# Attention scores: products over 96 stacked rows of the whole array in place of 64-row tiles

## What is computed

```python
x = x + tanh(g_xattn[0]) * L0_xattn(layernorm(x), ctx, mask, ...)
x = x + tanh(g_ffn[0])   * L0_ffn(layernorm(x), ...)     # mixture of 8 experts, top 2, and a shared one
x = x + tanh(g_xattn[1]) * L1_xattn(layernorm(x), ctx, ...)
x = x + tanh(g_ffn[1])   * L1_ffn(layernorm(x), ...)     # ternary weights

# in either attention, 16 heads of 16 numbers
Q = q @ Wq + bq;  K = ctx @ Wk + bk;  V = ctx @ Wv + bv
attn = softmax(Q K^T / 4 + mask);  out = (attn V) @ Wo + bo
```

## Time and profile before

| | |
|---|---|
| median of 3 runs | 1268.31 us (1262.6 to 1273.34) |
| the profiled execution's span | 1276.2 us |
| TensorE busy | 1203.0 us, 94% |
| VectorE busy | 998.5 us, 78% |
| ScalarE busy | 786.4 us, 62% |
| GpSimd busy | 673.1 us, 53% |
| share of the chain that ended last | PE 73%, DVE 10%, issue 7%, ACT 5%, POOL 4% |
| score matmuls (L832) in the two lines that the page has of q_hi's | 512 of them, mean 366 ns |

### The profile page before, as it was taken

The page is one execution under the profiler, slowest core; times in us unless marked ns, Lnnn a source line. Parts: engine busy times, 40 slices in busy tenths (PEclk is TensorE's granted clock), DMA queues, the critical chain, the costliest instruction groups (busy, mean ns, idle before and its releaser), DMA issues.

```text
span 1276.2 us, 27021 instructions
## 1 busy us (share of the span) xinstructions
PE 1203.0 (94%) x9168; PEld 1111.4 (87%) x9169; DVE 998.5 (78%) x2077; ACT 786.4 (62%) x1521; POOL 673.1 (53%) x772
## 2 busy tenths in 40 slices
PE   7999999989888999999799999999999999899998
PEld 6888888879878999999788888888899998788887
DVE  6888888866797676666668888887887788878887
ACT  4777677658554555555557767776444445677874
POOL 5333333333104555553777777730465466778885
PEclk8999999979899999999869999999999999999999
DMA  3221112023201333333533333302100000000000
GB/s 104 62 61 53 51 51 51 19 66 108 75 1 38 114 107 103 108 104 97 123 65 64 60 63 60 60 23 84 38 2 0 0 0 1 2 25 25 25 25 33
DMA packets 72319, 68.67 MB, mean 54 GB/s; under 512 B 26624, under 2 KB 64256, under 8 KB 72000
## 3 DMA queue, kind: packets, MB, share of 16 engines
q1 hardware_dynamic: 57936, 47.78, 12.5%
q0 software_dynamic: 12576, 18.62, 7.9%
q10 hardware_dynamic: 1744, 1.50, 0.4%
HBM read 44.00 MB, written 18.61 MB: 49 GB/s over the span
## 4 chain that ended last, share of the span: by engine, by line
PE 73%; DVE 10%; issue 7%; ACT 5%; POOL 4%; DMA 0%; ACTq 0%; DVEq 0%; POOLq 0%
PE PSUM L772 13%; PE PSUM L774 13%; PE PSUM L773 12%; PE PSUM L832 6%; PE PSUM L853 6%; PE PSUM L841 4%; PE PSUM L785 3%; PE PSUM L851 2%; PE PSUM L808 2%; PE PSUM L862 2%; POOL s_t_gh L2614 2%; PE PSUM L1914 1%; DVE s_a_q_lo L422 1%; ACT s_a_q_hi L677 1%; PE PSUM L2803 1%
## 5 line engine op out<-in xcount | busy, mean ns | idle before, releaser
L2164 POOL TENSOR_TENSOR s_f_h_lo<-s_f_h,s_f_h_hi 128x512 fp32r<-128x512 f32 x64 | 93.4, 1466 | 104.6 <-ACT s_f_h_hi L2108 104.0
L1337 POOL DMA_INDIRECT s_m_tile_x<-normed_x,s_tokens x78 | 95.7, 1227 | 77.0 <-DVE s_tokens L1628 55.5
L853 PEld LDWEIGHTS PSUM<-s_a_v_diagonal,s_a_prob_t 128*128 128x128 f32 x1024 | 128.4, 195 | 0.0
L853 PE MATMUL PSUM<-s_a_v_diagonal,s_a_prob_t 128*128 128x36 f32 x1024 | 127.4, 271 | 0.0
L1005 POOL DMA_INDIRECT s_x<-sorted_y,s_slots x60 | 95.1, 1586 | 50.2 <-DMA s_x<-sorted_y,s_slots 34.0
L454 DVE TENSOR_REDUCE s_a_row_max<-PSUM 128x8 f32<-128x640 f32 x128 | 104.4, 815 | 12.9 <-PE PSUM L832 10.3
L702 ACT ACTIVATE s_a_prob_t<-PSUM 128x640 f32<-128x640 f32 x128 | 89.4, 699 | 34.2 <-PE PSUM L841 33.4
L832 PE MATMUL PSUM<-s_a_kd,s_a_q_hi 64*128 64x320 f32 x512 | 92.8, 366 | 16.7 <-DVE s_a_q_lo L422 16.7
L461 DVE TENSOR_TENSOR s_a_less<-PSUM,s_a_row_max 128x640 f32<-128x640 f32 x128 | 105.0, 820 | 3.6 <-issue 0.2
L685 ACT ACTIVATE s_a_prob<-s_a_less 128x512 f32<-128x512 f32 x128 | 80.5, 629 | 41.8 <-DVE s_a_less L461 41.7
L2102 ACT ACTIVATE s_f_h<-PSUM,s_cols 128x512 f32<-128x512 f32 x64 | 44.0, 688 | 89.0 <-PE PSUM L774 88.3
(11 more groups left out here) (327 smaller groups left out, 4318.4 us busy)
## 6 DMA issues: line engine op xcount, KB each, us to landing
sorted_y<-s_m_tile_y SPq DMA_DIRECT2D x39, 256.0 KB, 2.1
s_a_kd<-s_a_k_parts SPq DMA_DIRECT2D x252, 20.0 KB
s_x<-x SPq DMA_DIRECT2D x16, 256.0 KB, 2.8
s_a_ctx<-ctx SPq DMA_DIRECT2D x32, 128.0 KB, 2.5
s_moe_raw<-moe_w SPq DMA_DIRECT2D x16, 256.0 KB, 3.4
normed_x<-s_m_xn SPq DMA_DIRECT2D x16, 256.0 KB, 3.2
y<-s_x SPq DMA_DIRECT2D x16, 256.0 KB, 2.1
s_late_raw<-moe_w SPq DMA_DIRECT2D x11, 256.0 KB, 2.8
```

Source lines behind the costliest of these rows:

```text
L853: last = pe.matmul(a.o_ps[:, 2 * c:2 * c + 2, :], a.prob_t[j % 2][:, c, :], v[:, j // BT, 0, 2 * c:2 * c + 2], start=False, stop=c == PC - ...
L1337: pool.indirect_dma_start(m.tile_x[n % 2][:, t, :], None, d["normed_x"], bass.IndirectOffsetOnAxis(ap=tokens[:, BT * n + t:BT * n + t + 1] ...
L2164: pool.tensor_tensor(f.h_lo[m % 4][:], f.h[m % 4][:], f.h_hi[m % 4][:].bitcast(F32), ALU.subtract).then_inc(f.h_split, 1)
```

## The change

1. **Layout.** `lay_out` permutes the columns of Wq and Wk (and their biases), so that four neighbouring partitions of a chunk hold the same row of its four head pairs.
2. **Stacks.** A new buffer `q_stack` has in 96 partitions three copies of a head pair's 32 rows: q_hi, q_lo, q_hi. `kd` has in the same 96 partitions k_hi, k_hi, k_lo, the two heads of a pair in columns of their own. The three products hi x hi, lo x hi and hi x lo are so one contraction over 96 rows. `q_stack` is filled by three DMAs of 256 KB a block from SyncE (`stack_queries`), two from q_hi and one from q_lo; `kd` by six DMAs of 40 KB instead of eight of 20 KB. q_hi and q_lo have one buffer each instead of two.
3. **Score.** Four matmuls a unit, each 96 rows, 128 queries, 160 columns (one head pair), in place of six. Only j = 0 waits for the stacks (one semaphore, nine DMAs).
4. **Keys two blocks ahead.** The keys are made two blocks ahead, the values still one ahead. The second block's keys are made in the opening. x is still loaded two blocks ahead.
5. **Order.** The bodies of all engines are reordered. TensorE's turn: tp(last,3), score 1, wv(last,2), transpose_x of the next, tp 0, score 2, wv(last,3), queries of the next, wv 0, score 3, tp 1, transpose_o of the last, a wait for the next block's q_lo, keys of the block after next, values of the next, tp 2, wv 1, score 0 of the next, and project of the last, which waits for both parts of the next block's value matrix and for the keys' parts. The `reach` of the loops on TensorE and ScalarE is 3, so two more blocks are unrolled.

The lines that carry it, left out: semaphore names, buffers' places in memory, the bodies of ScalarE and GpSimd.

```diff
+
+    row = np.arange(P) // 4
+    chunk_order = (2 * (np.arange(P) % 4) + row // HD) * HD + row % HD
+    by_pair = np.concatenate([m * P + chunk_order for m in range(KC)])
+    i = {**i, "L0_xattn_Wq": i["L0_xattn_Wq"][by_pair], "L0_xattn_Wk": i["L0_xattn_Wk"][by_pair],
+         "L1_xattn_Wq": i["L1_xattn_Wq"][:, by_pair], "L1_xattn_Wk": i["L1_xattn_Wk"][:, by_pair],
+         **{n: i[n][by_pair] for n in ("L0_xattn_bq", "L0_xattn_bk", "L1_xattn_bq", "L1_xattn_bk")}}
...
-                    self.kd = [sb(scope, n + f"kd{z}", [P, 2, KC, HPC // 2, CTXP], F32R) for z in two]
+                    self.kd = [sb(scope, n + f"kd{z}", [P, 2, HEAD_PAIRS, KC, CTXP], F32R) for z in two]
...
-        def spread_keys(engine, a, b, heads):
+        def spread_keys(engine, a, b, places):
             engine.wait_ge(a.k_split, b.count + 1)
-            for h in heads:
-                rows = slice(h * HD, (h + 1) * HD)
-                engine.dma_start(a.kd[b.z][rows, :, :, h % (HPC // 2), :].bitcast(F32),
-                                 a.k_parts[b.z][rows].bitcast(F32)).then_inc(a.kd_in[b.z], 16)
+            for h in places:
+                for copy, part in enumerate((0, 0, 1)):
+                    rows = slice(copy * PAIR_ROWS + h * HD, copy * PAIR_ROWS + (h + 1) * HD)
+                    engine.dma_start(a.kd[b.z][rows, h].bitcast(F32),
+                                     a.k_parts[b.z][h * P // 2:(h + 1) * P // 2, part].bitcast(F32)).then_inc(a.stacks_in[b.z], 16)
+
+        def stack_queries(engine, a, b):
+            stack = a.q_stack[b.z]
+            engine.wait_ge(a.q_round, b.count + 1)
+            for copy in (0, 2):
+                engine.dma_start(stack[copy * PAIR_ROWS:(copy + 1) * PAIR_ROWS].bitcast(F32), a.q_hi[:].bitcast(F32)).then_inc(a.stacks_in[b.z], 16)
+            engine.wait_ge(a.q_split, b.count + 1)
+            engine.dma_start(stack[PAIR_ROWS:2 * PAIR_ROWS].bitcast(F32), a.q_lo[:].bitcast(F32)).then_inc(a.stacks_in[b.z], 16)
...
                 late_rows = a.stage == 1 and not behind
-                if ahead and (a.stage or behind):
-                    ln_apply(b.next())
                 if a.stage and ahead == 0:
                     ffn_norm(0)
+                score_max(b, 1)
                 if behind:
                     normalise(b.last(), 2)
-                score_max(b, 1)
                 less_max(b, 1)
+                if ahead:
+                    x_residue(b.next())
                 if ahead > 1 and not late_rows:
                     ln_stats(b.next().next())
                 if a.stage and ahead == 1:
                     ffn_stats()
                 if a.stage and ahead == 0:
                     ffn_norm(1)
-                if ahead:
-                    keys(b.next())
-                if ahead:
-                    value_tails(b.next())
                 if behind:
                     normalise(b.last(), 3)
+                score_max(b, 2)
+                less_max(b, 2)
+                normalise(b, 0)
+                if ahead:
+                    q_residue(b.next())
                 if ahead > 1 and not late_rows:
                     ln_aggregate(b.next().next())
                 if a.stage and ahead == 1:
                     ffn_aggregate()
-                score_max(b, 2)
-                less_max(b, 2)
-                normalise(b, 0)
-                if ahead:
-                    x_residue(b.next())
+                score_max(b, 3)
                 if behind:
                     o_residue(b.last())
-                score_max(b, 3)
+                if ahead > 1:
+                    keys(b.next().next())
+                less_max(b, 3)
+                if ahead:
+                    value_tails(b.next())
+                if a.stage and ahead == 0:
+                    ffn_residue()
+                normalise(b, 1)
                 if late_rows:
                     ln_stats(second.next())
                     ln_aggregate(second.next())
                 if ahead:
-                    q_residue(b.next())
-                less_max(b, 3)
-                if a.stage and ahead == 0:
-                    ffn_residue()
-                if ahead:
                     score_max(b.next(), 0)
-                normalise(b, 1)
-                if ahead:
                     less_max(b.next(), 0)
                 if behind:
                     residual(b.last())
+                if ahead > 1:
+                    ln_apply(b.next().next())
...
                 if opens(a, b):
-                    act.wait_ge(first_steps, 2)
+                    act.wait_ge(a.first_k_ps, 1)
+                elif isinstance(b.n, int) and b.n == 0:
+                    act.wait_ge(a.v_ps, b.count + 1)
+                elif isinstance(b.n, int) and b.n == 1:
+                    act.wait_ge(a.first_k_ps, 2 + a.stage)
                 else:
-                    act.wait_ge(a.kv_ps, b.count + 1)
-                after(act, a.kd_in[b.z], 16 * HPC * (b.half + a.base // 2))
+                    act.wait_ge(a.v_ps, b.count)
+                after(act, a.stacks_in[b.z], 16 * STACK_DMAS * (b.half + a.base // 2))
                 for m in range(KC):
                     last = act.activation(a.k_parts[b.z][:, 0, m, :], k_bank(a, b)[:, m * CTXP:(m + 1) * CTXP], ACT.Identity,
                                           bias=cols[:, a.bk + m:a.bk + m + 1])
                 last.then_inc(a.k_round, 1)
 
...
             def q_rounded(b):
                 act.wait_ge(a.q_ps, b.count + 1)
+                if not (isinstance(b.n, int) and b.n == 0):
+                    stacked = b.last()
+                    act.wait_ge(a.stacks_in[stacked.z], 16 * STACK_DMAS * (stacked.half + a.base // 2 + 1))
                 for m in range(KC):
-                    last = act.activation(a.q_hi[b.z][:, m, :], q_bank(a, b)[:, m * SEQ:(m + 1) * SEQ], ACT.Identity,
+                    last = act.activation(a.q_hi[:, m, :], q_bank(a, b)[:, m * SEQ:(m + 1) * SEQ], ACT.Identity,
...
             def score(b, j):
                 u = UNITS * b.count + j
                 m, qt = j // BT, j % BT
-                pe.wait_ge(a.kd_in[b.z], 16 * HPC * (b.half + a.base // 2 + 1))
-                pe.wait_ge(a.q_split, b.count + 1)
+                if j == 0:
+                    pe.wait_ge(a.stacks_in[b.z], 16 * STACK_DMAS * (b.half + a.base // 2 + 1))
                 pe.wait_ge(a.masked, u + 1)
-                queries = (a.q_hi[b.z], a.q_lo[b.z], a.q_hi[b.z])
-                keys = (a.kd_hi[b.z], a.kd_hi[b.z], a.kd_lo[b.z])
-                for i in range(3):
-                    for c in range(2):
-                        rows = slice(c * P // 2, (c + 1) * P // 2)
-                        ps = a.scores[:, j % 2, c, 0:HPC // 2 * CTXP].rearrange("p (h n) -> p h n", n=CTXP)
-                        last = pe.matmul(ps, queries[i][rows, m, qt * P:(qt + 1) * P], keys[i][rows, m],
-                                         start=False, stop=i == 2, skip_group_check=True)
+                for p in range(HEAD_PAIRS):
+                    ps = a.scores[:, j % 2, p // 2, p % 2 * 2 * CTXP:(p % 2 + 1) * 2 * CTXP].rearrange("p (h n) -> p h n", n=CTXP)
+                    last = pe.matmul(ps, a.q_stack[b.z][0:STACK, p, m, qt * P:(qt + 1) * P], a.kd[b.z][0:STACK, :, p, m, :],
+                                     start=False, stop=True, skip_group_check=True)
                 last.then_inc(a.scores_ps, 1)
...
 
                 if ahead:
-                    pe.wait_ge(a.q_split, b.count + 3)
+                    pe.wait_ge(a.v_main, b.count + 3)
+                    pe.wait_ge(a.v_tail, b.count + 3)
+                    if ahead > 1:
+                        pe.wait_ge(a.k_split, b.count + 4)
                 else:
                     pe.wait_ge(a.y_done, b.count + 1)
...
                 if behind:
                     transpose_prob(b.last(), 3)
+                score(b, 1)
+                if behind:
                     weigh_values(b.last(), 2)
-                score(b, 1)
                 if ahead:
-                    keys_values(b.next())
-                if behind:
-                    weigh_values(b.last(), 3)
-                else:
+                    transpose_x(b.next())
+                if not behind:
                     pe.wait_ge(a.bias_step, 4 + 3 * a.stage)
                 transpose_prob(b, 0)
                 score(b, 2)
+                if behind:
+                    weigh_values(b.last(), 3)
                 if ahead:
-                    transpose_x(b.next())
+                    queries(b.next())
                 weigh_values(b, 0)
+                score(b, 3)
                 transpose_prob(b, 1)
-                score(b, 3)
                 if behind:
                     transpose_o(b.last(), 1)
                 if ahead:
-                    queries(b.next())
+                    pe.wait_ge(a.q_split, b.count + 2)
+                if ahead > 1:
+                    keys(b.next().next())
+                if ahead:
```

(7 more changed lines are left out.)

160 lines of the change are left out of this document (95 added, 65 removed).

## The result

The changed kernel takes 1420.81 us, the kernel before 1265.49 in the same runs (the 1268.31 above is the median of three of its four): a ratio of 1.1208 (95% interval 1.1162 to 1.1254). 1262 was forecast, with a range up to 1288.

A forecast was written before the change was run, and what follows sets the result against it. TensorE was taken to bound the turn, 15.08 us of work plus a 0.42 wait. Steady turns -12.7, last turns -2, openings +4.6 and clock +4 gave -6.1, so 1268.3 became 1262 us, range 1246 to 1288.

The forecast's parts named there:

- Score unit 0.45: TensorE's four-matmul score unit: 0.45 us instead of 0.76, four units a turn, so 1.24 us less work a turn.
- D: Rival on TensorE's scores: 160 columns run at the slow rate, 1.07 us a unit, turn 16.5, about 1305 us; chance 0.11.
- Turn 15.01, with waits of 0.34 and 0.83: Steady attention turn: 13.84 us work, waits 0.34 for q_lo before keys, 0.83 for value tails before project; -0.49 a turn.
- The last two turns of a stage, taken as 1 us shorter: Each attention stage's last two blocks, without queries or keys, get no new wait: about -1 us a stage, -2 together.
- So up to 4.3 us after q_lo it is hidden: cost 0.: Query-stack DMAs in the turn: landing up to 4.3 us after q_lo is covered by TensorE's other work, cost 0.
- E: Rival on the stack DMAs: landing later than 4.3 us after q_lo; 5 us gives turn 15.7, about 1280 or more; chance 0.03.
- Openings +2.3 each: Start of both attention stages: a transfer now lies between q_lo and the first score, +2.3 us each, +4.6 together.
- Clock +4: TensorE's clock in first turns: longer idle and thinner work may bring more low clock, 0 to +17 us, taken as +4.
- C: Rival on TensorE's clock: low level for longer, 1267 to 1275 us, up to 1290 with further terms; chance 0.14.

The follow-up runs named there:

- four-row kernel: Changed kernel with copy c of row r at partition 4r + c, contraction over 128 rows, each fourth zero: 1267.52 us, 1.0005 of before.
- second trace of before: The kernel before, unchanged, run once more for another trace: 1264.01 us at a granted clock of 0.991, with turns of 15.50 us.

## Why the prediction was wrong

- **Score unit 0.45.** 0.49 measured, and the weight loader's idle time ahead of it is gone. Right; D (1.07 a unit) fell.
- **Turn 15.01, with waits of 0.34 and 0.83.** Without the landing it is 14.86, with 0.25 and 0.63. Right in its parts, a little long: the chain for the value tails was 0.2 shorter than its parts laid end to end. The error of the unit went the other way: with 0.49 the work is 14.00 and not 13.84, and 14.00 + 0.25 + 0.63 = 14.88. The last two turns of a stage, taken as 1 us shorter, are 0.4 longer in stage 0 and 1.8 in stage 1 (four-row kernel against the second trace of before).
- **"So up to 4.3 us after q_lo it is hidden: cost 0."** This step failed. The bound of 2.1 to 3.4 us came from single transfers of the same size between memory and all 128 partitions (the 2.1 out of them, the 3.4 into them). Here three come together and each writes 32 neighbouring partitions, and the last lands after 6.7 us. The slack that was worked out, 4.3 us, was right: in the turn shown it is 3.6 and the 0.63 of the second wait, and the kernels whose stacks go through in 2.2 to 2.4 us show next to no wait. The text even had the rule that spoke against it, and priced it for one transfer, as 1.2 us. Three at that rate are already an estimated 3.6; at the measured 144 GB/s one takes 1.8 us, and the three follow one another.
- **E at 0.03, and at 15.7 us a turn.** The case that came true was priced at a landing of 5 us and without the clock. In stage 0 the wait beyond the value tails is 2.5 us a turn, the low clock behind it 3.0. Of the 155 us between the spans of the changed and the four-row kernel, 144 lie in the turns from the first transpose_o of a stage to its last, near 5.5 x 26 = 143; the rest is around the openings.
- **Openings +2.3 each.** From the end of q_lo to the first score it was 0.26 us before. It is 3.0 and 4.3 in the two stages of the four-row kernel, and 7.5 and 7.0 in the changed one: the same landing again, and too small a term even without it.
- **Clock +4.** The mechanism was right and is seen in the four-row kernel. Against the second trace of before, its turns from the first transpose_o of a stage to the last are 7.8 and 8.0 us shorter, but the way to the first is 5.5 longer, that between the stages 10.2, the end 2.6. Of these 18.3 us, 6.8 are the two openings. The rest fits the clock: its mean of 0.971 instead of 0.991 is about 50 us more at the lower level, and the two traces of before, which do the same work, differ by about 55 such us and by 13.9 us of span; that gives an estimated 12 us. The size was too small, in part because the trace of before had a low stretch that its second trace does not have.
- **A slip in the sum of C.** 1279 and 15.6 are 1294.6, not 1290. Nothing rests on it.

Had the landing been as assumed, the time would have lain in the range: 1264.36 and 1267.52 for the two kernels in which it does. That these are so near 1262 is in part luck. The four-row kernel gains nothing (1.0005) where 0.5% was forecast: its turns gain more than the sum had, and openings, last turns and clock take all of it back.

## What to carry to other kernels

A landing time belongs to a pattern: take it from a transfer that writes the same partitions and stands in the same queue behind the same others, and if there is none, let the range run to all of them one behind the other. When a tile is filled by partial transfers, spread each over every third or fourth partition, if the layout of a contraction leaves the order of its rows free. And a wait on TensorE is priced with some of the work behind it at half the clock, until a row shows otherwise: turns with waits of 0.25 and 0.63 us stayed at 1.00, those with 1.16 us did in some places and not in others.

## What the runs showed of the hardware

- Three transfers of 256 KB from SBUF to SBUF in packets of 2 KB: 144 GB/s onto 32 neighbouring partitions, 243 onto each third, 334 to 352 onto each fourth or onto all. The first 50 packets take near 88 ns each in every pattern, the slow ones too.
- Idle times of 2.8 to 4.1 us ahead of the score came with 3 to 7 us at half the clock, up to 14 in the first turns, in all of the loops' turns but one; matmuls without a use, put in their place, took 61 us off. Waits of 1.2 us came with it in most turns of one kernel and not in all.
- Four matmuls of 160 columns in the rounded format cost 0.49 us with 96 rows and no more with 128.
